# Four projection banks, an earlier head sum, moved weight preparation and re-dealt lookups in the first batch of an attention and feed-forward kernel

## The reference

```python
def _ln(t, w, b):                         # over the 32 columns of a head
    ...
q = _ln((x @ Wq + bq).reshape(b, s1, H, HD), qn_w, qn_b)
k = _ln(kv[..., :HD], kn_w, kn_b);  v = kv[..., HD:]
ctx = _attn(q, k, v) + _attn(q, k_dca, v_dca)      # softmax(q k^T / sqrt(32)) v
x = x + ctx @ Wo + bo
...
w = lut[idx]                              # gate_idx, up_idx (1376 x 512), down_idx (512 x 1376)
h = silu(layernorm(x) @ w_gate.T) * (layernorm(x) @ w_up.T)
x = x + h @ w_down.T
```

## Time and profile before

| what | us |
|---|---|
| median of three runs | 919.49 |
| lowest and highest | 918.78, 923.66 |
| the profiled execution | 919.11 |
| its span in the trace | 917.3 |
| first batch: start to first scores | 0 to 78.3 |
| scores and shift | 78.3 to 176.3 |
| second stage and last lookup | 176.3 to 245.5 |
| batches 1 to 3 and the last feed-forward | 245.5 to 917.3 |

### The profile page before, as it was taken

How to read it: one execution, slowest core, us unless ns; L and a number is a source line. 1 busy time by engine, 2 the same in 40 slices (tenths; PEclk the granted TensorE clock), 3 DMA queues, 4 the chain that set the end, 5 groups by cost and what they waited for, 6 DMA issues and landing times.

```text
span 917.3 us, 15590 instructions
## 1 busy us (share of the span) xinstructions
PE 804.1 (88%) x5892; PEld 320.9 (35%) x5892; DVE 521.6 (57%) x934; ACT 487.0 (53%) x960; POOL 237.1 (26%) x280
## 2 busy tenths in 40 slices
PE   3683666599989999999999999999999999979998
PEld 1231222233345333332444333334443332234443
DVE  6847999788564798221646884216468940052220
ACT  2444677677534688565246885662468856521100
POOL 3764200000146322100463221003642210002330
PEclk9886788799999999999999999999999999998999
DMA  8327953244400000111100000101000000000001
GB/s 274 86 79 210 294 162 106 84 142 132 151 0 1 1 2 1 35 36 38 59 1 1 1 2 7 64 24 46 1 1 1 1 23 25 24 24 1 1 2 44
DMA packets 45167, 50.12 MB, mean 55 GB/s; under 512 B 6048, under 2 KB 33184, under 8 KB 45088
## 3 DMA queue, kind: packets, MB, share of 16 engines
q1 hardware_dynamic: 43536, 48.71, 17.8%
q10 hardware_dynamic: 1552, 0.37, 0.2%
HBM read 40.61 MB, written 8.45 MB: 53 GB/s over the span
## 4 chain that ended last, share of the span: by engine, by line
issue 32%; PE 31%; DVE 15%; POOL 14%; ACT 5%; DMA 1%; ACTq 1%; POOLq 0%; DVEq 0%
PE ps L1089 20%; POOL hrstd L497 7%; DVE arena L761 5%; DVE nmax L899 4%; PE ps L1279 3%; PE ps L1262 3%; POOL arena L462 3%; ACT ps L646 2%; PE ps L1235 2%; POOL arena L460 1%; POOL xrstd L467 1%; ACT arena L671 1%; PE ps L1135 1%; DMA wf_lo<-in_lut 1%; PE ps L1268 1%
## 5 line engine op out<-in xcount | busy, mean ns | idle before, releaser
L1089 PE MATMUL ps<-arena,wf_hi 128*128 128x512 f16 (+1 forms) x704 | 212.3, 384 | 4.6 <-DVE arena L814 1.7
L646 ACT ACTIVATE ps<-ps,nmax 128x496 f32<-128x496 f32 x256 | 165.2, 646 | 64.0 <-DVE arena L900 62.9
L671 ACT ACTIVATE arena<-ps 128x1024 f32<-128x1024 f32 x128 | 125.4, 1023 | 83.4 <-PE ps L1268 83.3
L899 DVE TENSOR_REDUCE nmax<-ps 128x2 f32<-128x992 f32 x128 | 151.5, 1184 | 22.4 <-PE ps L1235 22.3
L1089 PE MATMUL ps<-arena,wf_lo 128*128 128x512 f16 (+1 forms) x352 | 134.4, 382 | 0.0
L497 POOL TENSOR_TENSOR hrstd<-hvar,mhalf 128x16 f32<-128x16 f32 x32 | 94.5, 2953 | 132.1 <-DVE hvar L842 132.1
L1089 PE MATMUL ps<-wf_hi,arena 128*128 128x512 f16 (+1 forms) x352 | 114.1, 380 | 2.9 <-POOL arena L462 2.8
L1135 PE MATMUL ps<-arena,wf_lo 128*32 128x512 f16 (+1 forms) x1056 | 76.7, 433 | 27.3 <-ACT wf_lo L575 26.4
L1089 PEld LDWEIGHTS ps<-arena,wf_hi 128*128 128x128 f16 (+1 forms) x704 | 66.7, 101 | 93.4 <-DVE arena L768 11.0
L761 DVE TENSOR_SCALAR arena<-arena,wf_lo 128x2048 f16<-128x2048 f16 (+1 forms) x132 | 90.4, 746 | 5.8 <-PE ps L1135 2.8
L467 POOL TENSOR_TENSOR xrstd<-xvar,mhalf 128x1 f32<-128x1 f32 x32 | 18.1, 565 | 262.7 <-DVE xvar L797 262.6
(11 more groups left out here) (133 smaller groups left out, 1026.6 us busy)
## 6 DMA issues: line engine op xcount, KB each, us to landing
arena<-idx SPq DMA_DIRECT2D x124, 128.0 KB, 2.7
arena<-in_x SPq DMA_DIRECT2D x32, 256.0 KB, 2.8
wf_lo<-in_idx SPq DMA_DIRECT2D x10, 512.0 KB, 6.6
out<-arena SPq DMA_DIRECT2D x16, 256.0 KB, 2.0
idx<-wf_hi SPq DMA_DIRECT2D x10, 384.0 KB, 4.4
wf_lo<-in_idx SPq DMA_DIRECT2D x11, 256.0 KB, 7.0
arena<-in_ctxT SPq DMA_DIRECT2D x4, 512.0 KB, 4.9
arena<-in_Wq SPq DMA_DIRECT2D x4, 256.0 KB, 5.4
```

Source lines behind the costliest of these rows:

```text
L646: last = act.activation(sc, sc, ACT.Exp, bias=nmax[:, 0, t, h:h + 1], accum_out=den[:, 0, t, h:h + 1])
L671: act.activation(probs[n_ % 2][:, 2 * p:2 * p + 2, :], ps[:, bank:bank + 2, :], ACT.Exp).then_inc(s["probs_set"], 1)
L899: dve.tensor_reduce(nmax[:, 0, t, 2 * p:2 * p + 2], sc[:, :, DCA:S], AX_X, ALU.max, negate=True)
L1089: last = pe.matmul(dst, l, r, start=(first and i == 0), stop=(stop and i == len(todo) - 1))
```

## The change

- `proj_bank` has four banks in the first batch (`first`), two in the later ones. `project(u)` of the first batch waits for `normalise(u - 4)`. The banks of the first x turns move (`LB0`).
- DVE does `variance(u + 1)` ahead of `normalise(u)`. The code is shared, so this holds in all batches. POOL's `rstd(u)` waits in addition for `normalise(u - 2)`.
- Twelve small DMAs (norm parameters, value biases, table) go from ACT's queue to SP's, behind Wkv_dca and ahead of the indices.
- wv high goes on ACT from slot 0 to between two `query_hi`. Centring of Wk goes from DVE to POOL (`keys_centred`), its sum ahead of the bias halves on DVE. wv low on POOL goes from slot 1 to slot 0, the two additions for the table's unit matrices to `selectors`, `lookup_constants` to slot 3, and the two early `convert` to slots 4 and 5. On DVE wk low moves to slot 0, and the sum of Wkv_dca too.
- A dummy `Ln` is executed on ACT ahead of the wait for the denominators, in every batch.
- The 33 lookups are dealt anew. Before, one in each of 16 pairs, one in S_SHIFT, one in each of 16 steps. Now one in 11 pairs (none in pairs 1, 4, 7, 10, 13), one in S_SHIFT + 1, one in each step and a second one at n = 1, 4, 7, 10, 13. `next_x` stays.

```diff
-LOOKUP_SLOT = {slot: c for c, slot in enumerate(
-    [S_ONE + 2 * i + 1 for i in range(NQ)] + [S_SHIFT] + [S_TWO + n_ for n_ in range(G * T)])}
+LOOKUPS = {S_ONE + 2 * i + 1: 1 for i in range(NQ) if i % 3 != 1}
+LOOKUPS.update({S_SHIFT + 1: 1})
+LOOKUPS.update({S_TWO + n_: 1 + (n_ % 3 == 1) for n_ in range(G * T)})
+LOOKUP_FROM = {slot: sum(c for o, c in LOOKUPS.items() if o < slot) for slot in LOOKUPS}
...
-        LB0 = (FB, FB + 1, VB, VB + 1)
+        LB0 = (VB, VB + 1, TB, TB + 1)
...
-        proj_bank = lambda u: AB + (u + 1) % 2
+        proj_bank = lambda u, first: AB + (u % 4 if first else (u + 1) % 2)
...
@@ SP, behind Wkv_dca (and gone from ACT's queue)
+            for i, name in enumerate(("qn_w", "qn_b", "kn_w", "kn_b", "kn_dca_w", "kn_dca_b")):
+                sp.dma_start(st_ln[:, i, :], row(name, 0, HD).to_broadcast([P, HD])).then_inc(s["ln_in"], 16)
+            sp.dma_start(bvm, A["bv"]).then_inc(s["bv_in"], 16)
+            sp.dma_start(bvd, A["bvd"]).then_inc(s["bv_in"], 16)
+            for r in range(NR4):
+                sp.dma_start(lut_w[r * 32:(r + 1) * 32, :], ...).then_inc(s["lut_in"], 16)
...
@@ POOL
+            def keys_centred():
+                key = st_kv[0].rearrange("p (h d) -> p h d", d=HD)
+                pool.wait_ge(s["wk_sum"], 1)
+                link(pool.tensor_scalar(sum_k, sum_k, -1.0 / HD, 0.0, ALU.mult, ALU.add))
+                pool.tensor_tensor(key, key, sum_k.unsqueeze(2).to_broadcast([P, KC * H, HD]), ALU.add).then_inc(s["wk_cent"], 1)
...
                     pool.wait_ge(s["hsum_set"], nth(a, NU, u + 1))
+                    if u >= 2:
+                        pool.wait_ge(s["qn_set"], nth(a, NU, u - 1))
...
-                if slot == 1:
+                if slot == 0:
                     values_low()
...
-                if 3 <= slot < 3 + EARLY:
-                    convert(slot - 3)
+                if slot == 3:
+                    lookup_constants()
+                if 4 <= slot < 4 + EARLY:
+                    convert(slot - 4)
...
@@ ACT
+                act.wait_ge(s["S_exp"], nth(a, NS, NS))
+                act.activation(warm[:, :], sqs[0][:, 0, HD:SQ], ACT.Ln)
                 act.wait_ge(s["den_set"], nth(a, T, T))
-                act.wait_ge(s["S_exp"], nth(a, NS, NS))
...
             turn(1, 1, (0, 0), LB0[1])
+            act.wait_ge(s["wv_in"], 16)
+            act.activation(fl(wv[0]), st_kv[1], ACT.Copy, scale=WS).then_inc(s["wv_hi"], 1)
             query_hi(2)
...
@@ DVE
                 for u in range(NU + 1):
-                    if 1 <= u < NU:
-                        normalise(a, u)
                     if 1 <= u < NU - 1:
                         variance(a, u + 1)
+                    if 1 <= u < NU:
+                        normalise(a, u, prev is None)
...
@@ PE, project(u)
-                    if u >= 2:
+                    if prev is None:
+                        if u >= 4:
+                            pe.wait_ge(s["qn_set"], nth(a, NU, u - 3))
+                    elif u >= 2:
                         pe.wait_ge(s["qn_set"], nth(a, NU, u - 1))
```

More of the change, by code:

```diff
@@ L276, in _, with row @@
         def _(sp):
+            def row(name, lo, hi):
+                return A[name][lo:hi].rearrange("(o n) -> o n", o=1)
             def load_x(t, src, dst):
@@ L595, in tail, with square @@
                     turn(2, t, b, LB2[t])
-            def square(a, u):
+            def square(a, u, first):
                 act.wait_ge(s["proj_done"], nth(a, NU, u + 1))
@@ L600, in square @@
                     act.wait_ge(s["hsum_set"], nth(a, NU, u - 1))
-                act.activation(sqs[u % 2][:, :, 0:HD], heads(ps[:, proj_bank(u), :]), ACT.Square, scale=float(HD) ** -0.5).then_inc(s["sq_set"], 1)
+                act.activation(sqs[u % 2][:, :, 0:HD], heads(ps[:, proj_bank(u, first), :]), ACT.Square, scale=float(HD) ** -0.5).then_inc(s["sq_set"], 1)
             def core(a, between, nxt, prev):
@@ L717, in prepare @@
                     act.activation(fl(wo[0]), st_o, ACT.Copy, scale=WS).then_inc(s["wo_hi"], 1)
-                if LOOKUP_SLOT.get(slot, 0):
-                    lookup_out(LOOKUP_SLOT[slot] - 1)
+                for c in lookups_in(slot):
+                    if c:
+                        lookup_out(c - 1)
             core((0, 0), prepare, (0, 1), None)
@@ L842, in variance, with normalise @@
                 dve.tensor_reduce(hvar[:, i, :], sqs[i], AX_X, ALU.add).then_inc(s["hsum_set"], 1)
-            def normalise(a, u):
+            def normalise(a, u, first):
                 dve.wait_ge(s["hrstd_set"], nth(a, NU, u + 1))
@@ L847, in normalise @@
                     dve.wait_ge(s["tr_ps"], nth(a, NU, u - 1))
-                dve.tensor_tensor(heads(qn[u % 2]), heads(ps[:, proj_bank(u), :]),
+                dve.tensor_tensor(heads(qn[u % 2]), heads(ps[:, proj_bank(u, first), :]),
                                   hrstd[:, u % 2, :].unsqueeze(2).to_broadcast([P, H, HD]), ALU.mult).then_inc(s["qn_set"], 1)
@@ L1014, in _ @@
             dve.tensor_scalar(par[:, 0:2], par[:, 0:2], QK_SCALE, None, ALU.mult).then_inc(s["par_set"], 1)
-            normalise(first, 0)
             variance(first, 1)
+            normalise(first, 0, True)
             turn(1, 3, first, LB0[3])
@@ L1022, in prepare @@
             def prepare(slot):
-                key = heads(st_kv[0])
                 dk = st_d.rearrange("p k (n h d) -> p k n h d", n=2, d=HD)[:, :, 0]
                 if slot == 0:
-                    dve.wait_ge(s["wk_in"], 16)
-                    dve.tensor_reduce(sum_k, key, AX_X, ALU.add).then_inc(s["wk_sum"], 1)
-                    dve.wait_ge(s["wk_sum"], 1)
-                    dve.scalar_tensor_tensor(out=key, in0=spread(sum_k), scalar=-1.0 / HD, in1=key, op0=ALU.mult, op1=ALU.add)\
-                        .then_inc(s["wk_cent"], 1)
-                if slot == 1:
                     dve.wait_ge(s["wd_in"], 16)
                     dve.tensor_reduce(sum_d, dk, AX_X, ALU.add).then_inc(s["wd_sum"], 1)
+                    dve.wait_ge(s["wk_hi"], 1)
+                    low(fl(wk[1]), st_kv[0], fl(wk[0])).then_inc(s["wk_lo"], 1)
+                if slot == 1:
                     dve.wait_ge(s["wd_sum"], 1)
@@ L1046, in prepare @@
                     low(fl(wo[1]), st_o, fl(wo[0])).then_inc(s["wo_lo"], 1)
-                if slot in LOOKUP_SLOT:
-                    one_hot(LOOKUP_SLOT[slot])
+                for c in lookups_in(slot):
+                    one_hot(c)
             core(first, prepare, (0, 1), None)
@@ L1161, in project @@
                     cols = slice(t * P, (t + 1) * P)
[L1162 removed]
+                    if prev is None:
+                        if u >= 4:
+                            pe.wait_ge(s["qn_set"], nth(a, NU, u - 3))
+                    elif u >= 2:
                         pe.wait_ge(s["qn_set"], nth(a, NU, u - 1))
[L1164 removed]
+                    elif u == 1:
                         pe.wait_ge(s["aT_lo"], nth(prev, G, G))
@@ L1296, in _, with prepare @@
                 turn(1, t, (0, 0), LB0[t], x_first[t])
-            core((0, 0), lambda slot: look_up(LOOKUP_SLOT[slot] - 1) if LOOKUP_SLOT.get(slot, 0) else None, (0, 1), None)
+            def prepare(slot):
+                for c in lookups_in(slot):
+                    if c:
+                        look_up(c - 1)
+            core((0, 0), prepare, (0, 1), None)
             look_up(NCH - 1)
```

47 lines of the change are left out of this document (21 added, 26 removed).

## The result

| | before | after |
|---|---|---|
| median time, us (4 runs each) | 920.33 (918.78 to 923.66) | **933.45** (932.67 to 934.29) |
| after to before, ratio | | 1.0138, 95% interval 1.0107 to 1.0169 |
| profiled execution: time, span | 919.1, 917.3 | 933.2, 931.4 |
| first scores on PE | 78.29 | 76.85 |
| the turn of the shift on PE (`pe.transpose` of `caug`) | 175.73 | 162.73 |

The changed kernel is 1.4% slower: 13.1 us by the medians, 14.1 by the two spans. The two columns split the 14.1 by place: start and projections -1.4, scores and shift up to the turn -11.6, turn to first `scores_t` +3.0, second stage +24.2, all later batches -0.1.

A forecast was written before the change was run, and what follows sets the result against it. Before the later batches, POOL's powers and a late weight half pace the projections, DVE the scores, PE the second stage. On 919.1 us, +0.8 - 8 + 0.3 + 15.5 + 5.5 + 2.0 = +16.1 gave 935 us, range 925 to 942.

The forecast's parts named there:

- two tile terms: Second stage: x tile 2 comes late, so DVE and PE wait, +5.5 us; tile 3, with one more step, +2.0 us.
- the stage term +0.8: Start and projections of the first batch: gains and delays nearly cancel, +0.8 us, from -3 to +2.5.
- milder: Rival, second stage: x tiles arrive in time or their wait falls into PE's stalls, 926.5 us; chance 0.17.
- sign (1): Start, in the changed profile: first `query_low` near 9 us, the third near 18.
- Scores, -8 forecast: Scores: five pairs without a lookup relieve DVE, 9.2 us in sum, 6.6 at PE's lower clock; -8 taken.
- sign (3): Scores, in the changed profile: pairs without a one-hot 3.5 to 4.2 us apart.
- Shift, -2.4 forecast: Shift: without the lookup in S_SHIFT, ACT's table load for Ln starts 2.4 us earlier.
- The second lookup of a step, 3.1 forecast: Second stage: 1.2 us waiting for ACT to empty result banks plus 1.9 for the lookup; five cost +15.5 us.
- sign (5): Second stage: double steps of 6.8 us, PE waiting 1.2 us for ACT's second result copy between the lookups.
- sign (6): Third norm: DVE waits about 5 us for a DMA of x, PE some 5 us for the one-hot after it.
- the head sum costs in every batch: Rival, later batches: `normalise` is 1.1 us late, 3 x 1.1 us or twice that, 938 to 942 us; chance 0.12.
- Faster: Rival: PE less full, lookups cost VectorE time only, under 1.4 us per moved lookup in second stage; 904.9 us, chance 0.05.

The follow-up runs named there:

- experiment 1: Changed kernel with the old dealing of the lookups: 919.0 us, ratio 0.9983 to the kernel before; kernel before with only the new dealing: 936.2 us, 1.0178.
- Experiment 2: Changed kernel with x tiles 2 and 3 issued after the 17th and 21st repeated chunk, not the 22nd and 25th: 926.9 us, 1.0071 to the kernel before.
- experiment 4: Kernel of Experiment 2 with the first lookup of each two-lookup step put ahead of the weighted values: 928.6 us, 1.0096 to the kernel before.

## Why the prediction was right, point by point

Forecast 935.0, range 925 to 942; measured 933.45. The mechanism and the sign held: the dealing carries the loss, each second lookup costs 3.1 us, and the late tile is there. The sum of +16.1 stood against +14.1 by the spans. That it came so close is in part luck, since terms were off in both directions: start and projections by -2.2, scores, shift and turn by about -1, second stage by +1.2, with its two tile terms off by +2.3 and -2.0. Three small slips stand in the working: the stage term +0.8 has parts that add to +1.0, tile 2's own numbers give 4.8 to 5.3 where "5 to 6" and 5.5 were taken, and "milder" takes the scores at -9.2 where the forecast has -8.

- **Start and projections, +0.8 forecast, -1.4 measured.** In the sign (1), the first `query_low` came at 8.71 (near 9 forecast), but the third at 15.25 and not near 18. The step that failed is Wv's landing: 16.3 by the kernel before, 13.6 after (13.4 to 14.7 in the other traces with this conversion in its new place). ACT, to set beside the earlier trace rows:

```profile
13.64 1.06 ACT L718 ACTIVATE wv<-arena 128x1024 f16<-128x1024 f32 x1 [1.40 <-DMA arena<-in_Wv]
14.61 1.13 ACT L711 ACTIVATE wq<-arena 128x512 f16<-128x512 f32 x2
```

  I had 1.5 us of this only as the lower end of the range, and it was 2.7. The keys came at 47.25 (49 forecast), the last power ended at 71.6 (73 to 74 forecast). But the size of this term is not certain either: the kernel before with the new dealing has the start of the kernel before word for word, and its first scores stood at 76.54, not 78.29. Two executions of the same code differ there by 1.75 us, so that -1.4 can't be told from the forecast by one pair of traces. In the same way six traces with the changed start have the keys anywhere from 47.16 to 49.01. The ratio of experiment 1 gives a like bound, 1.6 us for all edits but the dealing.
- **The powers and keys.** The earlier trace rows has the keys waiting 6.71 us; after the change they wait 11.61, all of it for wd low on DVE, since units 2 and 3 ran early and the fourth bank bought nothing else. That was forecast.

```profile
47.25 2.72 PE L1108 MATMUL ps<-wk,arena 128*128 128x512 f16 x6 [11.61 <-DVE wd L971]
```

- **Scores, -8 forecast.** From the first maximum of the first pair to that of the last, VectorE took 163.49 - 79.79 = 83.7 us before, 74.9 after, 82.75 with the old dealing alone: -8.8 or -7.9. A pair without a one-hot, with the next pair's first maximum and the scores on PE that it waits for:

```profile
113.47 1.18 DVE L922 TENSOR_REDUCE nmax<-ps 128x2 f32<-128x992 f32 x1
...
116.26 1.47 PE L1257 MATMUL ps<-arena 32*128 32x512 f16 x12 [2.84 <-ACT ps L667]
...
117.76 1.19 DVE L922 TENSOR_REDUCE nmax<-ps 128x2 f32<-128x992 f32 x1 [1.82 <-PE ps L1257]
```

  They are 4.29 us long in four places (3.5 to 4.2 in sign (3)) and 5.25 in pair 4 with wo low. Against the old dealing that is 2.65 in pair 4, as forecast, but 0.75 to 1.1 in the others, not 1.55: 6.3 us together, my end for the lower clock (6.6). These scores take 1.47 us behind 2.84 us of idle time, where they took 0.83, and PE's clock in the stretch fell from 0.78 to 0.72. The rest, 1.5, came from pair 2, 6.55 us long with the old dealing and 5.05 here; I had not counted it. So the sum was right with two terms off in opposite directions.
- **Shift, -2.4 forecast:** from that last maximum to the turn 12.24 us before, 9.50 after, -2.7. The moved lookup does this without the dummy Ln. The kernel before with the new dealing has no dummy; it takes 9.41 us, and its load starts beside DVE's last sum just as after the change (159.61 and 159.62 there). The Ln itself begins 1.30 us behind the load's start there and 1.40 with the dummy, so the 0.1 us that I gave it shows as a loss:

```profile
160.41 1.28 ACT L663 ACT_TABLE_LOAD   x1
160.43 0.42 DVE L883 TENSOR_REDUCE den<-arena 128x16 f32<-128x256 f32 x1 [0.48 <-ACT arena L689]
...
161.71 0.31 ACT L663 ACTIVATE den<-den 128x128 f32<-128x128 f32 x1
```

- **Turn to first `scores_t`, +2.8 forecast, +3.0 measured**, 3.06 of it the lookup at the lower clock. Not in my sum: the Exp table reload behind it, 1.28 us, for which `scores_t` of step 1 waited 1.34 (0.2 us net, as said above). I had looked at the load in front of Ln and not at the one behind it.
- **The second lookup of a step, 3.1 forecast.** With sign (5): 6.8 us with 1.2 of wait in two of the five steps; 7.4 to 8.0 in the others (step 7 with its tile in time), where the first lookup took 2.5 us, paced by the one-hot's pieces. The kernel before has longer steps in the same three places (4.28, 4.28 and 4.87), so by place the second lookup costs 3.1, 3.3, 3.1, 3.1 and 3.1. All five: 15.5 by experiments 1 and 2, 15.5 forecast. That DVE's one-hot is a limit beside ACT's copy (experiment 4) was not in the forecast.
- **x tile 2, +5.5 forecast.** DVE waited 4.89 and PE 4.79, as in sign (6), and the lookups behind it lost 2 x 1.7 to the clock, of which I had only 0.8 for slow pieces. 7.8 measured by the step. So the path was right, and the price of PE's clock behind the wait was missing. **x tile 3, +2.0 forecast, 0 measured:** no wait for it stands in the trace. The two terms together, 7.5, were 7.8 by the steps and 6.2 by the ratios.
- **Later batches, 0 forecast, -0.1 measured**, and the zero hides a small cost. What the rival "the head sum costs in every batch" described does happen: PE's third query projection waits 1.1 us longer for `normalise`. Before, then after:

```profile
268.81 2.76 PE L1089 MATMUL ps<-wq,arena 128*128 128x512 f16 x12 [0.71 <-DVE arena L848]
...
284.13 2.76 PE L1108 MATMUL ps<-wq,arena 128*128 128x512 f16 x12 [1.84 <-DVE arena L871]
```

  The next wait, at the keys, falls from 1.41 us to 0.55, so batch 1 loses 0.28 us (0.15 forecast) and the three batches 0.5. In this pair of traces 0.6 us come back late in the run, where PE happens to return sooner from the lower clock. From batch 1 on the thirteen traces have 671.0 to 673.1 us, so 0.5 us can't be seen in the times, and the rival's 3.3 us or more is out.
- **The other rivals.** "Milder" (926.5) needed the tiles in time. Experiment 2 made them so and stands at 926.9; with the scores at -8 that rival would have said 927.7. "Faster" needed a moved lookup under 1.4 us in the second stage; it was 3.1 or more.

## What to carry to other kernels

Work moved from one engine's full stretch to another engine's is priced at both ends by what is late next there, not by its duration: here 2.7 us of VectorE time gave back 0.7 to 1.1 us in four pairs (2.65 in the one where other work filled the gap) and took 3.1 us, because the receiving engine had no slack: its own 1.9 us, the wait for the one pair of result banks, and behind that wait the next one-hot. When an instruction that paces a fixed queue (a one-hot that releases a chunk copy, with a tile's load behind it) is moved, count every consumer in that queue again; two numbers in the queue's table were 6 to 7 us. And before a start is made faster, look whether waits are placed ahead of the first user of what they guard, and what the earlier start sends to a resource that is already full.
